# Three list scatters a tile and one gather, one base gather and one output transfer a body in the last nine static tiles

## What is computed

```python
route_c = jnp.argmax(pc, axis=-1)
dropped = _drop_mask(route_c, pmax_c, capacity)
scale_c = (pmax_c / jax.lax.stop_gradient(pmax_c))[:, None]
common = _expert_mix(h, route_c, W1c, b1c, W2c, b2c, EC) * scale_c
...
route_u = jnp.argmax(pu, axis=-1)
unique = _expert_mix(h, route_u, W1u, b1u, W2u, b2u, EU) * scale_u
out = common + dropped[:, None].astype(h.dtype) * unique
```

## Time and profile before

| | us |
|---|---|
| median of three runs | 1305.6 |
| span of the profiled execution | 1376.3 |
| PE busy in it | 1221.8 (89%) |
| DVE busy | 886.3 (64%) |
| POOL busy | 627.7 (46%) |
| ScalarE (ACT) busy | 558.6 (41%) |

### The profile page before, as it was taken

How to read it: one execution, slowest core, us unless ns; L and a number is a source line. 1 busy time by engine, 2 the same in 40 slices (tenths; PEclk the granted TensorE clock), 3 DMA queues, 4 the chain that set the end, 5 groups by cost and what they waited for, 6 DMA issues and landing times.

```text
span 1376.3 us, 33201 instructions
## 1 busy us (share of the span) xinstructions
PE 1221.8 (89%) x12722; PEld 1039.1 (75%) x12722; DVE 886.3 (64%) x1991; ACT 558.6 (41%) x959; POOL 627.7 (46%) x990
## 2 busy tenths in 40 slices
PE   5889999999999999999999997569995788899982
PEld 4667778778778778778877876468995778889882
DVE  5676776786786786786687686568873333445341
ACT  1234344344344344344334443234542344455540
POOL 4233333334544544544444444526325565565564
PEclk8899999999999999999999998869997899999996
DMA  6001211212312312322322212488764556667640
GB/s 202 28 21 41 74 38 44 76 56 78 119 59 78 120 59 77 119 60 78 114 65 76 94 46 74 165 299 269 246 230 127 171 193 204 221 217 278 216 129 25
DMA packets 84367, 168.03 MB, mean 122 GB/s; under 512 B 16446, under 2 KB 57701, under 8 KB 84208
## 3 DMA queue, kind: packets, MB, share of 16 engines
q1 hardware_dynamic: 70544, 139.88, 31.7%
q0 software_dynamic: 13664, 26.00, 5.3%
HBM read 123.83 MB, written 45.45 MB: 123 GB/s over the span
## 4 chain that ended last, share of the span: by engine, by line
PE 46%; DVE 24%; issue 13%; POOL 10%; ACT 2%; another core or an unknown queue 2%; DMA 1%; SPq 1%; DVEq 0%; POOLq 0%; ACTq 0%
PE h_ps L1676 10%; PE y_ps L1687 9%; DVE capped L995 4%; PE round_banks L591 3%; PE gen L553 3%; PE gen L511 3%; POOL sorted_d L235 3%; POOL PT L877 3%; DVE xn L1011 2%; PE round_banks L564 2%; DVE nm L999 2%; DVE nm L997 2%; PE gen L520 2%; POOL rstd L870 2%
## 5 line engine op out<-in xcount | busy, mean ns | idle before, releaser
L760 ACT ACTIVATE PT<-round_banks 128x1752 f32<-128x1752 f32 x96 | 156.7, 1633 | 174.5 <-PE round_banks L591 174.5
L877 POOL TENSOR_SCALAR_AFFINE_SELECT PT<-PT 128x512 f32<-128x512 f32 x192 | 118.1, 639 | 207.4 <-ACT PT L760 207.0
L1766 ACT ACTIVATE Gl<-h_ps,W 128x256 f32<-128x256 f32 x264 | 117.4, 476 | 230.5 <-PE h_ps L1676 160.2
L1676 PE MATMUL h_ps<-XH,Wh 128*128 128x256 f32 x528 | 156.3, 311 | 49.6 <-issue 26.6
L1687 PE MATMUL y_ps<-W,Gl 128*128 128x192 f32 x1056 | 188.9, 333 | 2.0 <-issue 2.0
L1687 PEld LDWEIGHTS y_ps<-W,Gl 128*128 128x128 f32 x1056 | 177.7, 195 | 3.7 <-issue 3.7
L1676 PEld LDWEIGHTS h_ps<-XH,Wh 128*128 128x128 f32 x528 | 108.1, 205 | 56.6 <-issue 39.2
L511 PE MATMUL gen<-w_emb,xT 128*128 128x192 f32 (+1 forms) x768 | 143.6, 339 | 7.5 <-DMA ident<-in_ident_dram 7.5
L1676 PE MATMUL h_ps<-XH,Wl 128*128 128x256 f32 x528 | 145.9, 296 | 0.2 <-issue 0.2
L1576 POOL DMA_INDIRECT out_dram<-Y,sid x76 | 84.8, 1116 | 129.7 <-DVE Y L1859 105.0
L1835 DVE TENSOR_TENSOR Wl<-W,Wh 128x768 fp32r<-128x768 f32 x88 | 84.2, 958 | 84.0 <-ACT Wh L1746 45.8
(11 more groups left out here) (273 smaller groups left out, 2454.7 us busy)
## 6 DMA issues: line engine op xcount, KB each, us to landing
W<-in_experts_dram SPq DMA_DIRECT2D x44, 771.0 KB
W<-in_experts_dram SPq DMA_DIRECT2D x44, 672.0 KB
xT<-in_xT_dram SPq DMA_DIRECT2D x32, 591.0 KB
X<-sorted_d SPq DMA_DIRECT2D x35, 386.0 KB
stage<-rows_d SPq DMA_DIRECT2D x64, 192.0 KB
rows_d<-h SPq DMA_DIRECT2D x32, 192.0 KB
out_dram<-h SPq DMA_DIRECT2D x32, 192.0 KB
rows_d<-xn SPq DMA_DIRECT2D x32, 192.0 KB
```

The costliest lines, as they stand in the source:

```text
L760: act.activation(PT[(JG * b + j) % 2][:], R[:, :, 0:438], ACT.Exp, scale=SCALE).then_inc(exps, 1)
L877: pool.affine_select(x[:, :, at:at + P], x[:, :, at:at + P], [[0, GH], [1, P]], ALU.is_ge, 0.0, base=0, channel_multiplier=-1)
L1676: mm = pe.matmul(h_ps[f % 3][:, 0:ROWS], w[t.par][:, cols], x, start=(k == 0), stop=(k == len(products) - 1))
L1766: act.activation(Gl[t.par][:, f, :], h_ps[f % 3][:, 0:ROWS], ACT.Gelu, bias=W[t.i][:, B1O + f:B1O + f + 1]).then_inc(g_ready, 1)
```

## The change

1. `BEFORE`: the 72 list scatters, four a body in bodies 12 to 23 and three in bodies 24 to 31, become three a body in bodies 12 to 33, with a fourth in every fourth body (12, 16, 20, 24, 28, 32). SP's wait for them moves from body 32 to body 34 and is followed by the loads of lists 35, 36 and 37 in a row.
2. POOL's bodies from 34 on: the gathers of tiles 35 to 43 stand in bodies 34 to 40 (`GATHERED`; two each in 34 and 35); the outputs go out two bodies after their tile, and each base gather stands one body after its tile.
3. DVE: from body 37 on, `add_rest(t-2)` stands in every body t. Before, the additions of tiles 35 to 43 stood in bodies 36, 38, 40, 42 (two), 43 (two) and `finish` (two).

```diff
-SPREAD = PLACE + 1
-BEFORE = [sum(4 if n < SPREAD + 12 else 3 for n in range(SPREAD, t)) for t in range(FIXED - 2)]
+SPREAD, SPREAD_END = PLACE + 1, FIXED - 1
+BEFORE = [sum(4 if (n - SPREAD) % 4 == 0 else 3 for n in range(SPREAD, t)) for t in range(SPREAD_END + 1)]
...
+GATHERED = {SPREAD_END: (FIXED, FIXED + 1), FIXED: (FIXED + 2, FIXED + 3)} | {n: (n + 3,) for n in range(FIXED + 1, STATIC - 3)}
...
-                    if t.number == FIXED - AHEAD:
+                    if t.number == SPREAD_END:
 
                         sp.wait_ge(spread_out, 16 * COLS)
-                    if t.number is not None and FIXED <= t.number + AHEAD < STATIC:
-                        load_list(Tile((t.number + AHEAD) // DEPTH, (t.number + AHEAD) % DEPTH))
+                        for n in range(FIXED, SPREAD_END + AHEAD):
+                            load_list(static(n))
+                    if t.number is not None and SPREAD_END <= t.number < STATIC - AHEAD:
+                        load_list(static(t.number + AHEAD))
...
-                    if 3 <= t.number < FIXED + 3:
+                    if 3 <= t.number < FIXED + 1:
                         send(t.before(3))
-                    if t.number == FIXED + 2:
+                    for n in GATHERED.get(t.number, ()):
+                        cast(static(n))
+                        gather(static(n))
+                    if t.number == FIXED + 1:
+                        send(static(FIXED - 2))
+                        number(static(FIXED - 1))
+                        send(static(FIXED - 1))
                         fetch(static(FIXED))
-                    if FIXED - 2 <= t.number <= CT + 2:
-                        gather(static(t.number + 2))
-                    if FIXED - 3 <= t.number <= CT + 2:
-                        cast(static(t.number + 3))
-                    if t.number in (CT, CT + 1):
-                        send(static(t.number - 3))
-                        fetch(static(t.number - 2))
-                    if t.number == CT + 2:
-                        gather(static(CT + 5))
-                        send(static(CT - 1))
-                        for n in range(CT, CT + 4):
-                            fetch(static(n))
-                    if t.number == CT + 4:
-                        send(static(CT))
-                        send(static(CT + 1))
-                        fetch(static(CT + 4))
-                        fetch(static(CT + 5))
-                    if t.number == CT + 5:
-                        send(static(CT + 2))
-                        send(static(CT + 3))
+                    if FIXED + 2 <= t.number <= CT + 1:
+                        send(static(t.number - 2))
+                        fetch(static(t.number - 1))
+                    if CT + 2 <= t.number < STATIC:
+                        fetch(static(t.number - 1))
+                        if t.number == STATIC - 1:
+                            fetch(t)
+                        send(static(t.number - 2))
...
-                    if t.number in (FIXED + 1, CT, CT + 2):
-                        add_rest(static({FIXED + 1: FIXED, CT: CT - 2, CT + 2: CT - 1}[t.number]))
-                    if t.number in (CT + 4, CT + 5):
-                        add_rest(static(2 * t.number - CT - 8))
-                        add_rest(static(2 * t.number - CT - 7))
+                    if t.number is not None and t.number >= FIXED + 2:
+                        add_rest(t.before(2))
```

More of the change, by code:

```diff
@@ L1625, in body @@
-                if t.number is not None and 2 <= t.n < FIXED + 2:
+                    for n in GATHERED.get(t.number, ()):
[5 more added lines that the diff above has]
+                        send(static(FIXED - 1))
+                        fetch(static(FIXED))
+                    if FIXED + 2 <= t.number <= CT + 1:
+                        send(static(t.number - 2))
+                        fetch(static(t.number - 1))
@@ L1626, in body @@
+                    if CT + 2 <= t.number < STATIC:
[3 more added lines that the diff above has]
+                        send(static(t.number - 2))
+                if t.number is not None and 2 <= t.n < FIXED + 1:
                     number(t.before(2))
-                if t.number is not None and SPREAD <= t.number < FIXED - 3:
+                if t.number is not None and SPREAD <= t.number < SPREAD_END:
```

## The result

The changed kernel took 1312.95 us (median of 8 runs, 1307.33 to 1315.08), the kernel before 1304.22 us beside it (8 runs, 1302.53 to 1308.9). The ratio is 1.0047, 95% interval 1.0026 to 1.0067: 6.1 us slower (3.4 to 8.7), where 1.1 us was forecast. It lies on the edge of what the prediction called "same" (0.58) and "slower" (0.27): the ratio is just under its 0.5%, the median 0.8 us above its bound of 1312.1.

The account below looks back on a forecast made before the run. PE was taken to set the pace, 7.95 us a tile, with a tail of POOL behind it. The terms +0.8 +0.7 +4.8 -5.2 summed to +1.1 us, 1305.6 to 1306.7 us; range 1298 to 1315.

Parts of the forecast that it names:

- same: Outcome within 0.5% (6.5 us) of the kernel before, from 1299.1 to 1312.1 us; chance 0.58.
- slower: Outcome above 1312.1 us, from the long chain, upper bounds without gain at the end, or a late list; chance 0.27.
- The scatters at nothing: List scatters on POOL: fewer a body gain nothing, since they are hidden under PE's pace of 7.95 us a tile.
- the 70.7 us left out: Profiled span's 70.7 us above the median: the scatter stretch's 60.4 us taken as belonging mostly to that execution, not priced.
- The late gather, +0.8 us: Scatters ending in body 33 delay tile 35's first gather; PE waits 0.8 us, bounds 0 and 3.7.
- The chain, +4.8 us: Base, addition, output of tiles 36 to 38: links of 11.9 and 10.4 us make PE lose 4.8 us more.
- The sign that I had named: In the profile after, POOL's last transfers without a gap number over 12, not 16.
- The end, -5.2 us: POOL's last transfers: 12 instead of 16 left at the end, 4 x 1.308 = 5.2 us gained if PE is done.
- The long chain: Rival: the chain goes on to the end, tiles 39 to 41 each 2.45 us late, +7.3, so 1314.0; chance 0.24.
- scatters hold PE up: Rival: timed runs lose the scatter stretch's time too; -21 us, 1285.8, or half of it, 1296; chance 0.12.
- The hidden links: Rival: links hide under DVE's and PE's slack while the end gains: -5.2+0.8, so 1301.2; chance 0.16.
- The rule weighed: Skill's time for a GpSimd transfer, about 2.0 us plus bytes: 2.2 us here; by it the sum would be -1.7 us.

Follow-up runs that it names:

- the second profile of before: The kernel before, unchanged, profiled once more: span 1300.3 us, run time 1302.03 us.
- e3: Part 3 alone on the kernel before (additions of tiles 35 to 43 two bodies behind; scatters and POOL's order as before): ratio 0.9995.
- b3: Kernel before with addresses of tiles 36, 37 worked out ahead of outputs, gathers of 39 to 43 in POOL's waits, additions of 37 to 41 re-placed: ratio 0.9940.
- b2: b1 with the gathers of tiles 41 and 42 also moved ahead into POOL's waits: ratio 0.9983 to the kernel before.
- b1: Kernel before with tiles 38 and 39 added one at a time, in bodies 41 and 42 instead of both in 42: ratio 0.9981.

## Why the prediction was right or wrong, point by point

**The scatters at nothing, the 70.7 us left out: right.** Shown by the second profile of before: 7.94 us a tile with four scatters and with three.

**The late gather, +0.8 us: mis-sized, the largest error.** It measured 3.0 to 4.4 us in the runs, and 2.88 of waiting and 1.68 of half clock (5.76 - 4.08) in the trace. The last scatter, the list and the last transfer of tile 35's gather in the changed kernel:

```profile
1187.30 0.97 POOL L184 DMA_INDIRECT list_d<-meta,pos  x1 [0.30 <-issue]
1192.07 2.60 SPq L1459 DMA_DIRECT2D L<-list_d  x3
1196.42 1.05 POOL L1534 DMA_INDIRECT late_X<-rows_d,gid  x1 [0.30 <-issue]
```

The last scatter ended 10.72 us ahead of PE's need (1188.27 against 1198.99), as forecast (10.66). Behind it, the list was issued at 1192.07, 3.80 us after the scatter's end and not 2.54; the gather's rows were in use 4.40 us after its issue ended (1197.47 to 1201.87), not 3.6; cast to gather took 1.1, not 0.5. The wait stayed under its upper bound of 3.7; but the half clock behind the wait, which I had counted at tile 41, I had not counted here.

**The chain, +4.8 us: right in the rows, wrong in the price.** The wait for base 35 went, 36 to 38 wait (7.72, 7.61, 7.00; forecast some 8, 7, 5), the links (from one addition to the next) took 11.57 and 10.97 us (forecast 11.9 and 10.4), and from the transposes of tile 40 to those of tile 43 PE is 9.8 us over the pace (forecast 4.70 + 4.8 = 9.5). But e3 has the same waits and takes no longer. The step that failed is the first one, that PE bounds the last tiles. From the output of tile 37 on the bound is POOL, and the row that showed it was there: 14 transfers without a break. In the page's means POOL is busy 46%, and in the stretched profile its stream was broken by waits of 6.54 and 4.16 us; the undisturbed profile has one of 2.62. The sign that I had named, an unbroken run over 12 transfers, came out as one over 28.

**The end, -5.2 us: wrong for the same reason.** Twelve instead of sixteen transfers behind a layer of PE is no gain when POOL is already issuing without a break well before that layer: the transfers are only issued earlier or later in the same stream. What counts is when the stream starts and how many stand in it: 28 from the output of tile 37 after, 26 before. +4.8 and -5.2 were two errors of about one size; parts 2 and 3 together measured +1.7 us (-0.7 to +4.1), where the sum had +0.3. That they cancelled in the sum was luck; with only one of them the forecast would have lain some 5 us to one side.

**Accounting**, from the transposes of tile 34 in the two undisturbed profiles (1190.88 after; 1191.32 before): the output of tile 37 starts 70.6 us later against 63.5, +7.1, of which the late gather is 4.8 (tile 36 is turned at +20.7 against +15.9); the other 2.3 lie in the chain, where the wait for tile 35's output alone is 1.5 longer (3.31 against 1.79). The stream behind it lasts 39.5 against 36.5 us, +3.0: two transfers more, and longer ones, against a wait of 2.62. That is 10.1 us, about the difference of these two executions' own times (1311.93 and 1302.03), and more than the 6.1 of the timed runs: single executions differ by some us; the last section names a candidate.

**The rivals.** The long chain was closest in time (1314.0). Its ground, that POOL has no slack there, was right; its sign, waits at tiles 39 to 41, did not show, so its nearness is luck. That scatters hold PE up was wrong: both kernels run 7.94 us a tile there. The hidden links were right in effect: they are hidden, under POOL and not under DVE's and PE's slack.

**The rule weighed.** The Trainium skill (DMA: Bandwidth & Descriptors, "Anatomy of one DMA — SWDGE (gpsimd) path") gave an estimate of 2.2 us for these transfers. The base of tile 37 was in use 4.11 us after its second transfer started (1255.76 to 1259.87), so the trace stands above it again, beside 316 GB/s of traffic (1255 to 1260); with the fit's links the sum would have been further off. At the end, beside 39 GB/s (1290 to 1295), the base of tile 43 was in use 2.57 us after its second transfer started (1292.14 to 1294.71), near the estimate; no run varied the traffic by itself.

## What to carry to other kernels

Ask of every engine that is busy half the time whether it is busy all the time in the stretch that ends last: count its instructions from the last chain to the end, and if they follow one another without a wait, that engine is the bound there, and waits elsewhere cost nothing until they delay its start or break it. By the table, what counts is when such a stream starts, how many instructions stand in it and what interrupts it. b3, which works on its start, gained 7.8 us; b2, which only fills waits, gained nothing beyond b1. And where a profile is some per cent longer than the timed runs, take a second one before pricing a wait from it.

## What was not expected of the hardware

- One profiled execution of the kernel before was 76 us longer than another of the same code (1376.3 and 1300.3 us), most of it where lists are scattered. Why stays open.
- How long POOL waited for the same output (tile 35's two transfers) differs from execution to execution: 5.75 us and 1.79 in the two profiles of before, 5.27 in b1, whose code is the same up to there, 3.31 in the changed kernel. It moves the start of the stream, and so is a candidate for the spread of the timed runs (1297.6 to 1312.1 us for the kernel before); that was not tested. The two long waits stood beside 332 and 319 GB/s of traffic in the 4 us behind the issue, 1.79 beside 227 and 3.31 beside 189; no run varied it.
- On POOL a gather right behind the cast of its addresses starts 0.77 to 0.90 us after it, where others start 0.30 us after the one before: part 2 put all nine of them so. I had not counted it. Only the gather of tile 43 stands so within the stream; the others lie ahead of it.
